# Mixture of experts in one fused block: the experts' leftover rows in units of 32 instead of 64

## The chip, the cores and the metric

The kernel runs on one core of a Trainium2 chip, as one program. Its time is device time in microseconds (us), the median of three runs; less is better. Times inside the kernel come from one profiled execution. PE is the matrix engine, DVE the vector engine, ACT the scalar engine, POOL the GpSimd engine, SP the queue that issues most transfers.

## The reference, cut to what matters

x is (32, 64, 256), which is 2048 tokens of 256 numbers. All arithmetic is float32.

```python
gate = xn @ wg_W + wg_b + (cond @ gg_W + gg_b)      # 8 experts
cw = top-2 of softmax(gate), as a weight per expert
h1 = relu(x @ W1[e] + b1[e])                        # 256 -> 512
h2 = relu(h1 @ W2[e] + b2[e])                       # 512 -> 512
out_e = h2 @ W3[e] + b3[e]                          # 512 -> 256
m = sum over e of cw[e] * out_e
x = x + attention_1(m)                              # 16 heads of 64, tanh, causal
x = x + ffn(attention_2(x))                         # second attention, then a quantized layer
```

Every token goes through two of eight experts, so there are 4096 (token, expert) rows to compute. How many each expert gets is known only at run time.

## The kernel before

**Stages.** After a short set-up (gate, ranks of the rows, a slot for each row) the expert stage runs over tiles of 128 slots; then the two attentions and the quantized layer run over 16 token tiles. The change lies in the expert stage and in the slot arithmetic ahead of it.

**Tiles.** The program's length is fixed, so there must be enough tiles for the worst split of the 4096 rows. There are `FULL` = 33 full tiles with one expert each and `MIXED` = 3 mixed tiles, each of `UNITS` = 2 units of `UNIT` = 64 rows, every unit with its own expert. `SLOT_TILES` = 36 tiles in all. They run in program order by position; `mixed(p)`, `nth(p)` and `slot_tile(p)` translate a position. The mixed tiles are at positions 13, 14 and 15.

**A full tile** keeps weights as the stationary operand and streams the 128 rows: layer 1 is 8 matrix products (L766), layer 2 is 16 (L796), layer 3 is 4 (L830, rows stationary, 256 columns streamed). A float32 product appears as two records in the trace. `turn_x` (L745) transposes the gathered rows.

**A mixed tile** has the rows of a unit as the stationary operand (64 columns of the array) and streams that unit's weights, 512 or 256 columns. The two units have their own column groups of the array (`tile_position=(0, g * UNIT)`), at L760, L790 and L816. Biases differ by row, so DVE adds gathered bias rows (L1934, L1942) and PE transposes the sum back (L775, L805).

**Order on PE.** A step j of `expert_step` is layer 1 of tile j+1, `turn_x` of tile j+2, layer 2 of tile j, layer 3 of tile j-1, with `turn_h2(j - 1)` and `turn_h1(j + 1)` where those tiles are mixed.

**Order on DVE.** In step j, DVE copies the expert's W1 for tile j+2 out of the arena (`take_w1`, L1910; L1906 when mixed), its W2 for tile j+1 (`take_w2`, L1926; L1921 when mixed), does the second activation (`relu2`, L1951) and adds b3 (L1970). A mixed tile needs the copies once per unit. ACT copies W3 for the units (`take_w3`).

**Transfers.** SP loads the attention weights (4 MB, L556) into the space that the mixed tiles' copies use, so it waits for the third layer of the last mixed tile: `sp.wait_ge(y_ps, LAST_MIXED + 1)`. PE waits for them (`w1_loaded`) after step `LAST - 2`. POOL gathers x rows (four buffers) and the mixed tiles' bias rows.

Of the kernel before, what the change touches and what calls it, by code (L numbers as in the profile page):

```python
# [35 lines left out]
UNIT = 64  # L36
UNITS = P // UNIT
FULL = 33
# [7 lines left out]
def units_left(small):  # L46

    blocks = (TOPK * TOK + (EXP - small) * (UNIT - 1) - small) // P
    return UNITS * max(blocks - FULL, 0) + max(small - max(FULL - blocks, 0), 0)  # L50

MIXED = -(-max(units_left(small) for small in range(EXP + 1)) // UNITS)
HOST = -(-(TOPK * TOK - EXP * UNIT) // P)
# [18 lines left out]
XG = 4  # L73
# [8 lines left out]
ROWS = dict(bo=HID, bout=HID, bffn=HID, bc2=H2, delta=1)  # L82
# [39 lines left out]
def mixed(p):  # L122

    return FIRST_MIXED <= p <= LAST_MIXED

def nth(p):

    return p - FIRST_MIXED if mixed(p) else p if p < FIRST_MIXED else p - MIXED

def slot_tile(p):

    if p < EXP:
        return p
    if p < FIRST_MIXED:
        return HOST + p - EXP
    return FULL + nth(p) if mixed(p) else nth(p) - (FULL - HOST)

# [25 lines left out]
def build(nc, t_in, out):  # L166
    ctx = ExitStack()
    with ctx:
# [19 lines left out]
        half_rows = sb("half_rows", [P, half_n])  # L188
# [24 lines left out]
        y = sb("y", [P, HID])  # L213
        root_table = sb("root_table", [P, 1])

        col = lambda name: cols[:, col_off[name][0]:col_off[name][1]]
        row = lambda name: rows[:, row_off[name][0]:row_off[name][1]]
        half_row = lambda name: half_rows[:, half_off[name][0]:half_off[name][1]]
# [41 lines left out]
        count_i, full_i, up_i = (r(EXP).bitcast(I32) for _ in range(3))  # L260
        past_first, past_full, to_first, to_full, to_rest, jump = (r(EXP) for _ in range(6))
        seg, room, behind = r(3 * EXP + 1), r(1), r(EXP)
        rank, over_first, over_full = (r(TT, EXP) for _ in range(3))
        picked = [over_first, over_full]
        slot_f = r(TOPK, TT)
# [12 lines left out]
        r = Region(l1_weights, 0, 4 * L1_SIZE)  # L278
# [11 lines left out]
        starts, row_slot, row_segment = r(3 * EXP + 1), r(MIXED), r(MIXED)  # L290
        starts_le, row_starts_le = r(FULL, 3 * EXP), r(MIXED, 3 * EXP)
# [7 lines left out]
        w1_b, w2_b = r(KH, MID), r(KM, MID)  # L299
        w3_now = [r(KM, HID) for _ in range(UNITS)]  # L300
        h1_rows, h2_rows = r(MID), r(MID)
        b1_rows, b2_rows = ([r(MID) for _ in range(BIAS_BUFS)] for _ in range(2))
        w1_of, w2_of = (w1_now, w1_b), (w2_now, w2_b)
# [20 lines left out]
        x_in = r(HID)  # L324
        wq2, wk2, wv2 = r(KH, HID), r(KH, HID), r(KH, HID)
# [179 lines left out]
        b1_gathered = [sem(f"b1_gathered{n}") for n in range(BIAS_BUFS)]  # L505
        b2_gathered = [sem(f"b2_gathered{n}") for n in range(BIAS_BUFS)]
# [12 lines left out]
        def _(sp):  # L519
# [29 lines left out]
            for half in range(2):  # L549
                sp.dma_start(half_rows[half * SEQ:(half + 1) * SEQ, :],  # L550
                             t_in["half_rows"][half:half + 1, :].to_broadcast([SEQ, half_n])).then_inc(half_loaded, 16)
# [7 lines left out]
            sp.wait_ge(w1_set, SLOT_TILES)  # L559
            for dst, name in ((wq2, "wq2"), (wk2, "wk2"), (wv2, "wv2"), (wc1, "wc1"), (wout2, "wout2")):  # L560
                sp.dma_start(dst, t_in[name].rearrange("(k p) n -> p k n", p=P)).then_inc(l2w_loaded, 16)
# [16 lines left out]
        def _(pool):  # L578
# [17 lines left out]
            for half in range(2):  # L596
                if half:
# [6 lines left out]
            pool.iota(row_slot, pattern=[[P, MIXED]], base=FULL * P, channel_multiplier=1,  # L604
                      allow_small_or_imprecise_dtypes=True).then_inc(row_slot_set, 1)
            pool.wait_ge(ids_set, 1)

            for j in range(SLOT_TILES):
# [5 lines left out]
                if mixed(j - 2):  # L615
                    n = nth(j - 2)
                    if n == 0:
                        pool.wait_ge(row_expert_set, 1)
                        pool.wait_ge(setup_done, 1)
                        pool.wait_ge(fa_stored, 16)  # L620
                    if n >= BIAS_BUFS:
                        pool.wait_ge(h1r_set, n - BIAS_BUFS + 1)
                    pool.indirect_dma_start(
                        out=b1_rows[n % BIAS_BUFS], out_offset=None, in_=t_in["b1"],
                        in_offset=bass.IndirectOffsetOnAxis(ap=row_expert[:, n:n + 1], axis=0)).then_inc(b1_gathered[n % BIAS_BUFS], 16)
                if mixed(j - 4):
                    n = nth(j - 4)
                    if n >= BIAS_BUFS:
                        pool.wait_ge(h2r_set, n - BIAS_BUFS + 1)
                    pool.indirect_dma_start(  # L630
                        out=b2_rows[n % BIAS_BUFS], out_offset=None, in_=t_in["b2"],
                        in_offset=bass.IndirectOffsetOnAxis(ap=row_expert[:, n:n + 1], axis=0)).then_inc(b2_gathered[n % BIAS_BUFS], 16)
# [3 lines left out]
            for t in range(TT):  # L636
# [7 lines left out]
                for c in range(TOPK):  # L644
                    pool.indirect_dma_start(  # L645
                        out=yg[:, c, :], out_offset=None, in_=expert_out if t else expert_out[0:(LAST_MIXED + 1) * P, :],
                        in_offset=bass.IndirectOffsetOnAxis(ap=slot_of[:, c, t:t + 1], axis=0)).then_inc(y_gathered, 16)
# [13 lines left out]
            for t in range(TT - 3, TT):  # L661
# [3 lines left out]
                pool.tensor_tensor(x1_bias[t % 2], x1, row("bffn"), ALU.add).then_inc(x1_bias_set, 1)  # L665
# [3 lines left out]
        def _(pe):  # L669
# [78 lines left out]
            def layer1(j):  # L748
# [21 lines left out]
            def turn_h1(j):  # L770
# [3 lines left out]
                for m in range(KM):  # L774
                    last = pe.transpose(ps[:, 1, m * P:(m + 1) * P], h1_rows[:, m * P:(m + 1) * P], ident[:, :])  # L775
                last.then_inc(h1r_turned, 1)

            def layer2(j):
# [7 lines left out]
                if mixed(j):  # L786
                    for k in range(KM):
                        for g in range(UNITS):
                            part_ = slice(g * UNIT, (g + 1) * UNIT)
                            last = mm(ps[part_, 2, :], h1_t[j % 2][:, k, part_], w2_of[g][:, k, :],  # L790
                                      start=k == 0, stop=k == KM - 1, tile_position=(0, g * UNIT))
# [8 lines left out]
            def turn_h2(j):  # L800
# [3 lines left out]
                for m in range(KM):  # L804
                    last = pe.transpose(ps[:, 3, m * P:(m + 1) * P], h2_rows[:, m * P:(m + 1) * P], ident[:, :])  # L805
                last.then_inc(h2r_turned, 1)

            def layer3(j):
                if mixed(j):
# [3 lines left out]
                    for k in range(KM):  # L813
                        for g in range(UNITS):
                            part_ = slice(g * UNIT, (g + 1) * UNIT)
                            last = mm(ps[part_, 4, 0:HID], h2_t[j % 2][:, k, part_], w3_now[g][:, k, :],  # L816
                                      start=k == 0, stop=k == KM - 1, tile_position=(0, g * UNIT))
# [3 lines left out]
                if j == EXP:  # L821
# [295 lines left out]
            def end_out1(t):  # L1117
# [4 lines left out]
                mm(dst, first_row, row("bo"), start=True, stop=False)  # L1122
# [91 lines left out]
            def end_out2(t):  # L1214
# [4 lines left out]
                mm(dst, first_row, row("bout"), start=True, stop=False)  # L1219
# [122 lines left out]
        def _(act):  # L1342
# [37 lines left out]
            def relu1(j):  # L1380
# [6 lines left out]
                if j == EXP:  # L1387
# [23 lines left out]
            def take_w3(j):  # L1411
# [4 lines left out]
                act.wait_ge(y_ps, j)  # L1416
                for g in range(UNITS):
                    e = act.value_load(row_expert[g * UNIT:g * UNIT + 1, nth(j):nth(j) + 1], min_val=0, max_val=EXP - 1)
                    at = act.snap(e * E_SIZE + W3_AT)
                    last = act.copy(w3_now[g].rearrange("p k n -> p (k n)"), arena[:, bass.ds(at, KM * HID)])  # L1420
                last.then_inc(w3_set, 1)

            def store_y(j):
                act.wait_ge(y_set, j + 1)
                act.dma_start(expert_out[j * P:(j + 1) * P, :], y[:, :]).then_inc(y_stored, 16)
# [296 lines left out]
        def _(dve):  # L1722
# [87 lines left out]
            first_row, seg_of = excl[:, :, 0], [seg[:, n * EXP + 1:(n + 1) * EXP + 1] for n in range(3)]  # L1810
            start_of, blocks_end = [starts[:, n * EXP:(n + 1) * EXP] for n in range(3)], starts[:, 2 * EXP:2 * EXP + 1]
# [3 lines left out]
            step(ts(count_i, up_i, -UNIT, None, ALU.bitwise_and))  # L1815
            step.go(ts(seg_of[0], full_i, float(P), None, ALU.min))
            step(tt(seg_of[2], count_i, full_i, ALU.subtract))
            step.go(tt(seg_of[1], full_i, seg_of[0], ALU.subtract))
            step(tt(rank, ps[:, 2, 0:TT * EXP].rearrange("p (i e) -> p i e", e=EXP), excl.rearrange("p e i -> p i e"), ALU.add))
            step.go(dve.tensor_tensor_scan(starts, seg, scan_zero.rearrange("p e i -> p (e i)")[:, 0:3 * EXP + 1], 0.0, ALU.add, ALU.add))  # L1820
            step.go(tt(past_full, full_i, first_row, ALU.add))
            step(ts(past_first, first_row, float(P), None, ALU.add))
            step.go(ts(room, blocks_end, -1.0 / UNITS, float(FULL * UNIT), ALU.mult, ALU.add))
            step.go(stt(to_full, start_of[1], -float(P), start_of[0], ALU.add, ALU.subtract))
            step.go(tt(to_first, start_of[0], first_row, ALU.subtract))
            step.go(tt(to_rest, full_i, start_of[0], ALU.add))
            step(tt(over_first, rank, per_e(past_first), ALU.is_ge))
            step.go(stt(behind, start_of[2], blocks_end, room.to_broadcast([P, EXP]), ALU.subtract, ALU.min))
            step.go(stt(jump, seg_of[0], 1.0 / P, to_full, ALU.mult, ALU.mult))
            step(tt(over_full, rank, per_e(past_full), ALU.is_ge))  # L1830
            step.go(stt(start_of[2], behind, 0.0, start_of[2], ALU.max, ALU.add))
            step.go(tt(to_rest, to_rest, jump, ALU.add))
# [615 lines left out]
```

## Time and profile before

| what | value |
|---|---|
| median of 3 runs | 742.73 us (741.77 to 743.66) |
| profiled execution, its own time | 744.68 us |
| span of its trace | 743.2 us |
| PE busy | 713.3 us (96%) |
| DVE, ACT, POOL busy | 65%, 39%, 12% |
| mean granted clock of PE | 0.986 of full speed |

The span runs from the first to the last instruction; the execution's own time holds what lies around it. A time by which a stage becomes shorter or longer can be taken from either.

### The profile page before, as it was taken

Reading aid. Unit: us, or ns where it says so; the run is one execution under the profiler, and the core shown is the slowest. Engines: PE = TensorE matmul, PEld = TensorE weight load, DVE = VectorE, ACT = ScalarE, POOL = GpSimd, SP = SyncE. Lnnn points to the kernel's source line nnn. Section 1 sums busy time; section 2 is a strip of 40 time slices with the busy share of each in tenths; the row PEclk is TensorE's granted clock in tenths of the full one; section 3 lists DMA queues with packets and bytes.
Section 4 is the critical chain, followed back from the end, with each engine's and each line's share of the span. In section 5 each row is a group of like instructions: output and inputs, shape, how many; then the busy total and the mean of one; then the engine's idle time right before and its main releaser. Section 6 shows DMA issues by size and latency. Waiting matters only on the chain.

```text
span 743.2 us, 20463 instructions
## 1 busy us (share of the span) xinstructions
PE 713.3 (96%) x8266; PEld 615.5 (83%) x8266; DVE 486.3 (65%) x1036; ACT 287.8 (39%) x839; POOL 90.9 (12%) x102
## 2 busy tenths in 40 slices
PE   6389999999999999999999999999999999999997
PEld 4279999559999999978778878978888897888785
DVE  4756565743545444334777787787778778777867
ACT  3032121142121221253465446445544654564552
POOL 2121112411111101031101101110110111000000
PEclk9599999999999999999999999999999999999999
DMA  7998111217111102310001000000110010000000
GB/s 262 336 353 322 37 37 56 81 43 257 50 37 37 37 30 69 118 50 23 16 9 30 30 7 25 30 23 10 30 31 9 23 30 24 8 16 16 9 9 23
DMA packets 21402, 49.13 MB, mean 66 GB/s; under 512 B 3323, under 2 KB 14971, under 8 KB 18749
## 3 DMA queue, kind: packets, MB, share of 16 engines
q1 hardware_dynamic: 12256, 32.47, 12.2%
q0 software_dynamic: 3744, 10.49, 4.7%
q10 hardware_dynamic: 5309, 4.87, 2.0%
q8 instruction: 66, 1.08, 0.6%
q14 instruction: 27, 0.22, 0.1%
HBM read 41.00 MB, written 6.82 MB: 64 GB/s over the span
## 4 chain that ended last, share of the span: by engine, by line
PE 94%; DVE 3%; ACT 1%; issue 1%; another core or an unknown queue 0%; DVEq 0%; POOL 0%; ACTq 0%; POOLq 0%
PE ps L897 16%; PE ps L796 15%; PE ps L766 8%; PE ps L923 8%; PE ps L830 7%; PE ps L982 7%; PE ps L948 4%; PE ps L998 3%; PE ps L941 2%; PE ps L973 2%; PE ps L1013 2%; PE ps L1075 2%; PE ps L1032 2%; PE ps L790 1%; PE ps L676 1%; PE ps L1045 1%
## 5 line engine op out<-in xcount | busy, mean ns | idle before, releaser
L897 PE MATMUL ps<-arena,l_weights 128*128 128x128 f32 x1024 | 125.9, 277 | 0.5 <-ACT arena L1470 0.5
L796 PE MATMUL ps<-h_t,w_now 128*128 128x128 f32 x1056 | 123.4, 275 | 1.2 <-DVE h_t L1951 1.2
L796 PEld LDWEIGHTS ps<-h_t,w_now 128*128 128x128 f32 x1056 | 120.5, 192 | 1.4 <-issue 1.4
L897 PEld LDWEIGHTS ps<-arena,l_weights 128*128 128x128 f32 x1024 | 119.3, 192 | 2.3 <-ACT arena L1470 1.0
L1395 ACT ACTIVATE h_t<-ps,cols 128x128 f32<-128x128 f32 x132 | 37.8, 367 | 163.9 <-PE ps L766 149.5
L1926 DVE COPY w_now<-arena 128x2048 f32 x33 | 40.5, 1227 | 83.2 <-PE ps L796 74.7
L1476 ACT ACTIVATE arena<-ps,cols 128x128 f32<-128x128 f32 x256 | 73.9, 387 | 48.0 <-PE ps L897 48.0
L645 POOL DMA_INDIRECT arena<-expert_out,slot_of x32 | 33.1, 1033 | 323.0 <-DVE arena L1979 272.8
L766 PEld LDWEIGHTS ps<-xg_t,w_now 128*128 128x128 f32 x528 | 63.4, 192 | 6.0 <-ACT xg_t L1378 3.5
L766 PE MATMUL ps<-xg_t,w_now 128*128 128x128 f32 x528 | 65.0, 276 | 3.0 <-ACT xg_t L1378 3.0
L612 POOL DMA_INDIRECT xg<-in_x,slot_tok x36 | 41.6, 1155 | 186.4 <-PE ps L745 157.4
L830 PE MATMUL ps<-arena,h_t 128*128 x264 | 62.5, 380 | 0.0
L923 PE MATMUL ps<-l_weights,arena 128*64 128x512 f32 x256 | 61.8, 605 | 0.0
L830 PEld LDWEIGHTS ps<-arena,h_t 128*128 128x128 f32 x264 | 47.7, 191 | 5.1
L982 PE MATMUL ps<-l_weights,arena 128*128 128x256 f32 x224 | 51.5, 383 | 0.0
L982 PEld LDWEIGHTS ps<-l_weights,arena 128*128 128x128 f32 x224 | 41.5, 190 | 5.2
L1910 DVE COPY w_now<-arena 128x1024 f32 x33 | 22.9, 694 | 29.3 <-PE ps L766 20.7
L1951 DVE TENSOR_SCALAR h_t<-ps,cols 128x128 f32<-128x128 f32 x128 | 35.8, 342 | 4.6 <-PE ps L796 4.5
L948 PE MATMUL ps<-ident,arena 128*128 128x128 f32 x256 | 38.3, 273 | 0.1
L2097 DVE TENSOR_TENSOR arena<-ps,half_rows 128x512 f32<-128x512 f32 x32 | 21.9, 686 | 22.7 <-PE ps L973 17.2
L923 PEld LDWEIGHTS ps<-l_weights,arena 128*64 128x64 f32 x256 | 15.6, 136 | 22.5 <-issue 21.4
L1559 ACT ACTIVATE arena<-arena 128x512 f32<-128x512 f32 x32 | 20.2, 631 | 31.6 <-DVE arena L2180 31.6
(366 smaller groups left out, 1097.1 us busy)
## 6 DMA issues: line engine op xcount, KB each, us to landing
arena<-in_experts SPq DMA_DIRECT2D x16, 1024.0 KB
expert_out<-y ACTq DMA_DIRECT2D x36, 128.0 KB
arena<-in_x_t SPq DMA_DIRECT2D x2, 1024.0 KB, 6.2
arena<-in_x SPq DMA_DIRECT2D x16, 128.0 KB
out<-arena SPq DMA_DIRECT2D x16, 128.0 KB, 1.7
b<-in_b SPq DMA_DIRECT2D x1, 1024.0 KB
l_weights<-in_wq SPq DMA_DIRECT2D x1, 1024.0 KB
l_weights<-in_wk SPq DMA_DIRECT2D x1, 1024.0 KB
```

What stands on the lines that cost most here:

```text
L612: pool.indirect_dma_start(out=xg[j % XG][:, :], out_offset=None, in_=t_in["x"], in_offset=bass.IndirectOffsetOnAxis(ap=slot_tok[:, slot_ti ...
L766: last = mm(ps[:, 0, m * P:(m + 1) * P], w1_now[:, k, m * P:(m + 1) * P], xg_t[:, k, :], start=k == 0, stop=k == KH - 1)
L796: last = mm(ps[:, 2, m * P:(m + 1) * P], w2_now[:, k, m * P:(m + 1) * P], h1_t[j % 2][:, k, :], start=k == 0, stop=k == KM - 1)
L830: last = mm(bank(4, HID), h2_t[j % 2][:, k, :], flat[:, bass.ds(at + k * HID, HID)], start=k == 0, stop=k == KM - 1)
L897: last = mm(ps[:, b, c * P:(c + 1) * P], wt[:, k, f:f + P], m_t[:, k, :], start=k == 0, stop=k == KH - 1)
L923: last = mm(ps[r * SEQ:(r + 1) * SEQ, value_bank(t, s), :], m_t[:, k, s * SEQ:(s + 1) * SEQ], wv[:, k, r * 512:(r + 1) * 512], start=k == ...
L948: last = pe.transpose(bank_[:, m * P:(m + 1) * P], p[:, h:h + 2, :], ident[:, :])
L982: last = mm(bank(1, HID), ctx_t[:, c, :], wo[:, c, :], start=c == 0, stop=c == C1 - 1)
L1395: last = f(h1_t[j % 2][:, k, :], ps[:, 0, k * P:(k + 1) * P], ACT.Relu, bias=cols[:, bass.ds(e * KM + at + k, 1)])
L1476: last = f(dst[:, cc, :], ps[:, project_bank(t, n), c * P:(c + 1) * P], ACT.Tanh, bias=col(bias)[:, cc:cc + 1])
L1926: dve.tensor_copy(w2_now[:, :, :].rearrange("p k n -> p (k n)"), arena[:, bass.ds(at, KM * MID)]).then_inc(w2_set, 1)
L1951: last = ts(h2_t[j % 2][:, k, :], ps[:, 2, k * P:(k + 1) * P], cols[:, bass.ds(e * KM + at + k, 1)], 0.0, ALU.add, ALU.max)
```

## The change

The leftover rows are handled in units of 32. There are 28 full tiles and 6 mixed ones, 34 in all. A mixed tile has three units, `UNIT_ROWS`: rows 0 to 63 (a couple, one expert), rows 64 to 95 and rows 96 to 127 (singles, each with an expert). Mixed tiles stand at positions 13, 16, 19, 22, 25 and 28. The couple's weights are copied where a tile's weights were before; the singles' weights are copied earlier, at the end of three steps (`spare_w1`, `spare_w2` twice). The slot arithmetic handles four segments rather than three. The bias rows have one buffer rather than two each, x rows three rather than four, and two small tables of rows (`half_rows`, `token_rows`) are loaded after the expert stage's last W1 copy.

```diff
-UNIT = 64
-UNITS = P // UNIT
-FULL = 33
+UNIT, COUPLE = 32, 64
+UNIT_ROWS = [slice(0, COUPLE), slice(COUPLE, COUPLE + UNIT), slice(COUPLE + UNIT, P)]
+FULL = 28
...
-FIRST_MIXED = EXP + FULL - HOST
-LAST_MIXED = FIRST_MIXED + MIXED - 1
-BIAS_BUFS = 2
+FIRST_MIXED = 13
+MIXED_POSITIONS = [FIRST_MIXED + 3 * n for n in range(MIXED)]
+LAST_MIXED = MIXED_POSITIONS[-1]
...
-XG = 4
+XG = 3
...
             def layer1(j):
...
                 if mixed(j):
+                    pe.wait_ge(spare_set, 3 * nth(j) + 1)
                     for k in range(KH):
-                        for g in range(UNITS):
-                            part_ = slice(g * UNIT, (g + 1) * UNIT)
+                        for g, part_ in enumerate(UNIT_ROWS):
                             last = mm(ps[part_, 0, :], xg_t[:, k, part_], w1_of[g][:, k, :],
-                                      start=k == 0, stop=k == KH - 1, tile_position=(0, g * UNIT))
+                                      start=k == 0, stop=k == KH - 1, tile_position=(0, part_.start))
...
             def expert_step(j):
...
                 if exists(j - 1, SLOT_TILES):
                     add_b3(j - 1)
+                spare_w1(j + 3)
+                spare_w2(j + 2, 1)
+                spare_w2(j + 1, 2)
...
+            def spare_w1(j):
+                if not mixed(j):
+                    return
...
+                experts_of[j] = [unit_expert(j, g) for g in range(len(UNIT_ROWS))]
+                for g in (1, 2):
+                    at = dve.snap(experts_of[j][g] * E_SIZE + W1_AT)
+                    last = dve.tensor_copy(w1_of[g].rearrange("p k n -> p (k n)"), arena[:, bass.ds(at, KH * MID)])
+                last.then_inc(spare_set, 1)
+
+            def spare_w2(j, g):
...
+                at = dve.snap(experts_of[j][g] * E_SIZE + W2_AT)
+                dve.tensor_copy(w2_of[g].rearrange("p k n -> p (k n)"), arena[:, bass.ds(at, KM * MID)]).then_inc(spare_set, 1)
...
-            step(dve.tensor_copy(slot_of[:, :, :], slot_f))
+            step(ts(past_split, slot_f, -float(SPLIT_AT), 0.0, ALU.add, ALU.max))
+            step.go(ts(shift_back, past_split, float(SPLIT * COUPLE), float(COUPLE - 2 * SPLIT * COUPLE), ALU.is_ge, ALU.mult))
+            step(ts(chunk_at, past_split, -COUPLE, None, ALU.bitwise_and))
+            step(tt(slot_f, slot_f, shift_back, ALU.add))
+            step(tt(slot_of[:, :, :], slot_f, chunk_at, ALU.add))
```

On PE, the second mixed tile of before (position 14, step 14) read as follows: its transposes, then layer 2 with `w_now` for one unit and `l_weights` for the other, both with 64 output rows.

```order
L745 MATMUL ps<-ident,xg 128x128 x2
L805 MATMUL ps<-ident,l_weights 128x128 x4
L790 MATMUL ps<-w_now,h_t 64x512
L790 MATMUL ps<-l_weights,h_t 64x512
L790 MATMUL ps<-w_now,h_t 64x512
L790 MATMUL ps<-l_weights,h_t 64x512
L790 MATMUL ps<-w_now,h_t 64x512
L790 MATMUL ps<-l_weights,h_t 64x512
L790 MATMUL ps<-w_now,h_t 64x512
L790 MATMUL ps<-l_weights,h_t 64x512
L775 MATMUL ps<-ident,l_weights 128x128 x4
```

The changed kernel has this at the first mixed tile (position 13, step 13):

```order
L774 MATMUL ps<-xg_t,w_now 128x128 x8
L753 MATMUL ps<-ident,xg 128x128 x2
L798 MATMUL ps<-w_now,h_t 64x512
L798 MATMUL ps<-l_weights,h_t 32x512 x2
L798 MATMUL ps<-w_now,h_t 64x512
L798 MATMUL ps<-l_weights,h_t 32x512 x2
L798 MATMUL ps<-w_now,h_t 64x512
L798 MATMUL ps<-l_weights,h_t 32x512 x2
L798 MATMUL ps<-w_now,h_t 64x512
L798 MATMUL ps<-l_weights,h_t 32x512 x2
```

Where products of one width followed each other, a product 64 wide and two 32 wide now alternate.

On DVE, the end of step 14 and the start of step 15 in the changed kernel hold the three-part b3 addition of tile 13 (L1999), a spare W2 copy for tile 16 (L1966), that tile's b1 addition (L1974) and the next copies (`w_now` is the tile's own weights, `l_weights` a spare):

```order
L1999 ISA
L1999 TENSOR_TENSOR y<-ps,b 32x256
L1966 ISA
L1966 COPY l_weights<-arena 128x2048
L1974 TENSOR_TENSOR mixed_rows<-ps,bias_rows 128x512
L1905 TENSOR_LOAD tile_expert
L1905 ISA x2
L1925 ISA
L1926 ISA
L1926 COPY w_now<-arena 128x1024
L1936 ISA
L1936 COPY w_now<-arena 128x2048
```

Before, the same kind of place (around the first mixed tile's b1 addition, L1934) had both units' copies one behind the other:

```order
L1934 TENSOR_TENSOR l_weights<-ps,l_weights 128x512
L1887 TENSOR_LOAD row_expert
L1887 ISA x2
L1887 TENSOR_LOAD row_expert
L1887 ISA x2
L1906 ISA
L1906 COPY w_now<-arena 128x1024
L1906 ISA
L1906 COPY l_weights<-arena 128x1024
L1921 ISA
L1921 COPY w_now<-arena 128x2048
L1921 ISA
```

A spare's copy moved from between the step's own work to the step's end.

## Rows read from the trace of the kernel before

**Rows 1.** The page, part 1: busy time of each engine

```profile
PE 713.3 (96%) x8266; PEld 615.5 (83%) x8266; DVE 486.3 (65%) x1036; ACT 287.8 (39%) x839; POOL 90.9 (12%) x102
```

**Rows 2.** Waits of PE, whole span: total, times, longest

```profile
PE ps L725 <- DVE arena L1860: 10.9, 2, 10.4
...
PE ps L766 <- ACT xg_t L1378: 3.0, 2, 1.7
...
PE ps L796 <- DVE h_t L1951: 1.2, 1, 1.2
```

**Rows 3.** Timeline, one step of full tiles: start, duration, engine, line

```profile
260.22 1.95 PE L766 MATMUL ps<-xg_t,w_now 128*128 128x128 f32 x16
...
262.23 3.74 PE L796 MATMUL ps<-h_t,w_now 128*128 128x128 f32 x32
...
265.80 1.89 PE L830 MATMUL ps<-arena,h_t 128*128 x8
266.30 1.23 DVE L1926 COPY w_now<-arena 128x2048 f32 x1 [3.19 <-PE ps L796]
...
267.53 1.95 PE L766 MATMUL ps<-xg_t,w_now 128*128 128x128 f32 x16
268.48 0.41 DVE L1970 TENSOR_TENSOR y<-ps,b 128x256 f32<-128x256 f32 x1
```

**Rows 4.** Windows: the five steps 12 to 16, with three mixed tiles

```profile
130.13:172.46 42.33, 41.10 (x268) 25.19 (x267) 24.10 (x38) 13.10 (x25) 11.93 (x9) 1.00 0.19 61
```

**Rows 5.** Timeline of PE and its weight loads, mixed tile at position 14

```profile
150.37 0.65 PE L790 MATMUL ps<-w_now,h_t 128*64 128x512 f32 x1
...
150.38 0.64 PE L790 MATMUL ps<-l_weights,h_t 128*64 128x512 f32 x1
...
153.00 0.59 PE L790 MATMUL ps<-w_now,h_t 128*64 128x512 f32 x1
...
153.43 0.59 PE L790 MATMUL ps<-w_now,h_t 128*64 128x512 f32 x1
...
153.96 0.42 PEld L775 LDWEIGHTS ps<-ident,l_weights 128*128 128x128 f32 x4 [0.81 <-issue]
...
154.55 1.95 PE L816 MATMUL ps<-l_weights,h_t 128*64 128x256 f32 x16
156.42 2.05 PE L766 MATMUL ps<-xg_t,w_now 128*128 128x128 f32 x16
```

**Rows 6.** Timeline: a change from 64-wide products to 64 by 64 tiles

```profile
407.74 1.03 PE L923 MATMUL ps<-l_weights,arena 128*64 128x512 f32 x4
408.70 0.32 PEld L973 LDWEIGHTS ps<-arena 64*64 64x64 f32 x16 [0.81 <-issue]
```

**Rows 7.** 32-wide products in four column groups: timeline; group over the span

```profile
7.38 1.07 PE L687 MATMUL ps<-arena 128*32 128x512 f32 x8
...
L1066 PE MATMUL ps<-arena 128*32 128x64 f32 x416 | 8.5, 222 | 0.0
```

**Rows 8.** Timeline of DVE in the slot arithmetic, where PE waits

```profile
22.67 0.16 DVE L1825 TENSOR_TENSOR arena<-l_weights,arena 128x8 f32<-128x8 f32 x1
22.75 0.16 DVE L1826 TENSOR_TENSOR arena<-arena,l_weights 128x8 f32<-128x8 int32 x1
...
24.25 0.28 DVE L1835 TENSOR_TENSOR arena<-arena 128x128 f32<-128x128 f32 x1
24.57 0.29 DVE L1836 TENSOR_TENSOR arena<-arena 128x128 f32<-128x128 f32 x1
...
26.47 0.18 DVE L1845 CAST slot_of<-arena 128x32 int32<-128x32 f32 x1
26.68 0.18 DVE L1850 TENSOR_SCALAR arena<-slot_of 128x32 int32<-128x32 int32 x1
```

**Rows 9.** SP's first issue of attention weights; transfer rates from 184 us, slices of 0.2 us

```profile
172.63 0.39 SPq L556 DMA_DIRECT2D l_weights<-in_wq  x1
...
GB/s 369 348 353 415 333 328 348 338 359 389 451 241 41 41 26 61 26 26 20 0 0 0 0 0 0 0 0 0 169 364 123 0 0 0 0 0 0 82 246 225
```

More of the change, by code:

```diff
@@ L122, in mixed, with out_block @@
 def mixed(p):
-    return FIRST_MIXED <= p <= LAST_MIXED
+    return p in MIXED_POSITIONS
 def nth(p):
-    return p - FIRST_MIXED if mixed(p) else p if p < FIRST_MIXED else p - MIXED
+    before = sum(at < p for at in MIXED_POSITIONS)
+    return before if mixed(p) else p - before
 def slot_tile(p):
[L135 to L139, printed above, removed]
+    return FULL + nth(p) if mixed(p) else nth(p)
+def out_block(p):
+    return p if p < EXP else EXP + nth(p) if mixed(p) else MIXED + nth(p)
 def later(t):
@@ L298, in build @@
         r = Region(l1_weights, 0, 4 * L1_SIZE)
[L299 to L303, printed above, removed]
+        w2_b, w2_c = r(KM, MID), r(KM, MID)
+        w3_of = [r(KM, HID), r(KM, HID), w3_c]
+        w1_b, w1_c = r(KH, MID), r(KH, MID)
+        w1_of, w2_of = (w1_now, w1_b, w1_c), (w2_now, w2_b, w2_c)
         class Blocks:
@@ L324, in build @@
         x_in = r(HID)
+        token_rows, half_rows = r(token_n), r(half_n)
         wq2, wk2, wv2 = r(KH, HID), r(KH, HID), r(KH, HID)
@@ L504, in build @@
         row_expert_set = sem("row_expert_set")
-        b1_gathered = [sem(f"b1_gathered{n}") for n in range(BIAS_BUFS)]
-        b2_gathered = [sem(f"b2_gathered{n}") for n in range(BIAS_BUFS)]
+        b1_gathered = sem("b1_gathered")
+        b2_gathered = sem("b2_gathered")
+        spare_set = sem("spare_set")
         w3_set = sem("w3_set")
@@ L559, in _ @@
             sp.wait_ge(w1_set, SLOT_TILES)
+            for half in range(2):
+                sp.dma_start(half_rows[half * SEQ:(half + 1) * SEQ, :],
+                             t_in["half_rows"][half:half + 1, :].to_broadcast([SEQ, half_n])).then_inc(half_loaded, 16)
+            sp.dma_start(token_rows, t_in["token_rows"].to_broadcast([P, token_n])).then_inc(half_loaded, 16)
             for dst, name in ((wq2, "wq2"), (wk2, "wk2"), (wv2, "wv2"), (wc1, "wc1"), (wout2, "wout2")):
@@ L664, in _ @@
                 pool.wait_ge(x1_bias_set, t)
-                pool.tensor_tensor(x1_bias[t % 2], x1, row("bffn"), ALU.add).then_inc(x1_bias_set, 1)
+                pool.tensor_tensor(x1_bias[t % 2], x1, token_row("bffn"), ALU.add).then_inc(x1_bias_set, 1)
         @block.tensor
@@ L813, in layer3 @@
                     for k in range(KM):
[L814 to L817, printed above, removed]
+                        for g, part_ in enumerate(UNIT_ROWS):
+                            last = mm(ps[part_, 4, 0:HID], h2_t[j % 2][:, k, part_], w3_of[g][:, k, :],
+                                      start=k == 0, stop=k == KM - 1, tile_position=(0, part_.start))
                     last.then_inc(y_ps, 1)
@@ L1121, in end_out1 @@
                 dst = bank(O_END[t], HID)
-                mm(dst, first_row, row("bo"), start=True, stop=False)
+                mm(dst, first_row, token_row("bo"), start=True, stop=False)
                 for c in range(C1):
@@ L1218, in end_out2 @@
                 dst = bank(OUT2_END[t], HID)
-                mm(dst, first_row, row("bout"), start=True, stop=False)
+                mm(dst, first_row, token_row("bout"), start=True, stop=False)
                 for c in range(C2):
@@ L1415, in take_w3 @@
                     act.wait_ge(moe_loaded[1], 16 * EXP)
-                act.wait_ge(y_ps, j)
-                for g in range(UNITS):
-                    e = act.value_load(row_expert[g * UNIT:g * UNIT + 1, nth(j):nth(j) + 1], min_val=0, max_val=EXP - 1)
+                if nth(j):
+                    act.wait_ge(y_ps, MIXED_POSITIONS[nth(j) - 1] + 1)
+                for g, part_ in enumerate(UNIT_ROWS):
+                    row_ = part_.start
+                    e = act.value_load(row_expert[row_:row_ + 1, nth(j):nth(j) + 1], min_val=0, max_val=EXP - 1)
                     at = act.snap(e * E_SIZE + W3_AT)
-                    last = act.copy(w3_now[g].rearrange("p k n -> p (k n)"), arena[:, bass.ds(at, KM * HID)])
+                    last = act.copy(w3_of[g].rearrange("p k n -> p (k n)"), arena[:, bass.ds(at, KM * HID)])
                 last.then_inc(w3_set, 1)
@@ L1886, in unit_expert @@
             def unit_expert(j, g):
-                return dve.value_load(row_expert[g * UNIT:g * UNIT + 1, nth(j):nth(j) + 1], min_val=0, max_val=EXP - 1)
+                row_ = UNIT_ROWS[g].start
+                return dve.value_load(row_expert[row_:row_ + 1, nth(j):nth(j) + 1], min_val=0, max_val=EXP - 1)
             def take_w1(j):
-                if j == EXP:
+                if nth(j) == EXP and not mixed(j):
                     dve.wait_ge(experts_set, 2)
@@ L1918, in take_w2 @@
                 if mixed(j):
-                    for g in range(UNITS):
-                        at = dve.snap(experts_of[j][g] * E_SIZE + W2_AT)
-                        last = dve.tensor_copy(w2_of[g][:, :, :].rearrange("p k n -> p (k n)"), arena[:, bass.ds(at, KM * MID)])
-                    last.then_inc(w2_set, 1)
+                    at = dve.snap(experts_of[j][0] * E_SIZE + W2_AT)
+                    dve.tensor_copy(w2_now[:, :, :].rearrange("p k n -> p (k n)"), arena[:, bass.ds(at, KM * MID)]).then_inc(w2_set, 1)
                     return
@@ L1926, in take_w2 @@
                 dve.tensor_copy(w2_now[:, :, :].rearrange("p k n -> p (k n)"), arena[:, bass.ds(at, KM * MID)]).then_inc(w2_set, 1)
+            def spare_w1(j):
+                if not mixed(j):
+                    return
+                if nth(j) == 0:
+                    dve.wait_ge(row_expert_set, 1)
+                    for n in range(2):
+                        dve.wait_ge(moe_loaded[n], 16 * EXP)
+                else:
+                    dve.wait_ge(l1_ps, MIXED_POSITIONS[nth(j) - 1] + 1)
+                experts_of[j] = [unit_expert(j, g) for g in range(len(UNIT_ROWS))]
[4 more added lines that the diff above has]
+            def spare_w2(j, g):
+                if not mixed(j):
+                    return
+                if nth(j) == 0:
+                    dve.wait_ge(setup_done, 1)
+                    dve.wait_ge(fa_stored, 16)
+                else:
+                    dve.wait_ge(l2_ps, MIXED_POSITIONS[nth(j) - 1] + 1)
+                at = dve.snap(experts_of[j][g] * E_SIZE + W2_AT)
+                dve.tensor_copy(w2_of[g].rearrange("p k n -> p (k n)"), arena[:, bass.ds(at, KM * MID)]).then_inc(spare_set, 1)
             def add_b1(j):
@@ L2128, in l1_bias_o @@
                 dve.wait_ge(o_ps, t + 1)
-                tt(o_rows, bank(1, HID), row("bo"), ALU.add).then_inc(ob_set, 1)
+                tt(o_rows, bank(1, HID), token_row("bo"), ALU.add).then_inc(ob_set, 1)
             def l1_residual(t):
@@ L2145, in l2_x1_bias @@
                     dve.wait_ge(fin_set, t - 1)
-                tt(x1_bias[t % 2], x1, row("bffn"), ALU.add).then_inc(x1_bias_set, 1)
+                tt(x1_bias[t % 2], x1, token_row("bffn"), ALU.add).then_inc(x1_bias_set, 1)
             def l2_z(t):
@@ L2218, in l2_bias_a @@
                 dve.wait_ge(a_ps, t + 1)
-                tt(a_rows, bank(6, HID), row("bout"), ALU.add).then_inc(a_set, 1)
+                tt(a_rows, bank(6, HID), token_row("bout"), ALU.add).then_inc(a_set, 1)
             def l2_scales(t):
@@ L2416 @@
         parity=np.stack([(np.arange(P) // D2 % 2 == odd).astype(np.float32) for odd in range(2)], axis=1))
-    rows = dict(bo=a(L0_attn_bo), bout=a(L0_cond2_bout),
-                bffn=a(L0_ffn_bias), bc2=a(L0_cond2_bc2)[order], delta=a(L0_ffn_delta_act))
+    token_rows = dict(bo=a(L0_attn_bo), bout=a(L0_cond2_bout), bffn=a(L0_ffn_bias))
+    rows = dict(bc2=a(L0_cond2_bc2)[order], delta=a(L0_ffn_delta_act))
     half_rows = dict(bv=a(L0_attn_bv).reshape(2, -1), bv2=bqkv[2].reshape(HALF, 2, D2).transpose(1, 0, 2).reshape(2, -1))
@@ L2432 @@
         "cols": join(cols, COLS, 1), "aug": join(aug, AUG, 1),
-        "rows": join(rows, ROWS, 0)[None], "half_rows": join(half_rows, HALF_ROWS, 1), "setup_rows": join(setup_rows, SETUP_ROWS, 0)[None],
+        "rows": join(rows, ROWS, 0)[None], "token_rows": join(token_rows, TOKEN_ROWS, 0)[None],
+        "half_rows": join(half_rows, HALF_ROWS, 1), "setup_rows": join(setup_rows, SETUP_ROWS, 0)[None],
         "we2_t": c(a(L0_cond2_We2).T), "ffn_w": c(a(L0_ffn_weight)), "ffn_dw": c(a(L0_ffn_delta_w).reshape(HID, NBLK)),
```

164 lines of the change are left out of this document (84 added, 80 removed).

## The prediction

> **What bounds the kernel now.** I read the busy shares first: PE is busy for 713.3 of 743.2 us [rows 1]. Then its waits: after the set-up almost nothing holds it. The one long wait, 10.4 us, is for DVE's slot arithmetic before any tile can start; two waits for the first gathered rows follow, and a single one of 1.2 us for DVE's activation in the expert stage [rows 2]. So two things count: how many PE microseconds the expert stage takes, and how long the slot arithmetic is. All other engines matter only where they come late for PE.
>
> The timeline of a step of full tiles shows what one costs: layer 1 starts at 260.22 and the next step's at 267.53, so 7.31 us a tile, with no gap on PE [rows 3]. The stretch with the mixed tiles took 42.33 us for five steps [rows 4]. Five full steps would be 36.55, so three mixed tiles cost 5.78 us more. PE's 1.23 us of idle time (42.33 minus 41.10 busy) is the wait of rows 2; the other 4.55 us are work, 1.52 us a mixed tile, mostly the transposes. The matrix products themselves are no dearer than a full tile's, because both units stream at once: the two records of L790 start at 150.37 and 150.38, and the next ones come 0.43 us apart (153.00, 153.43), which is a 512-column record [rows 5].
>
> **Fewer tiles.** 36 become 34: 2 x 7.31 = 14.6 us less [rows 3]. Three more tiles are mixed, 3 x 1.52 = 4.55 us more [rows 4]. The 1.2 us wait came from both units' copies standing ahead of a full tile's activation; that order is gone, so 1.2 us less, between 0 and that. Together -11.3 us if three units stream abreast as two do.
>
> **The slot arithmetic** lies on PE's long wait, so every operation added counts in full. Added are about five operations of 8 columns at 0.08 us (L1825 to L1826), three of 128 columns at up to 0.32 (L1835 to L1836), and four of 32 columns, three of them chained at 0.21 (L1845 to L1850) [rows 8]: 0.4 + 0.8 + 0.7 = 1.9 us. The bounds are 1.2 (all overlapped by half more) and 2.5.
>
> **Spare copies on DVE.** In a full step W2's copy starts 6.08 us after the step, lasts 1.23, then the activation and b3 follow until 8.7 (268.48 + 0.41 against 260.22) [rows 3]. A spare W2 copy behind that ends near 9.9 to 10.2. The tile ahead of a mixed one has its step lengthened to about 8.0 by `turn_h1`, and PE wants the spare 2.0 us (262.23 - 260.22) into the next one, at 10.0. So each of six mixed tiles may wait 0 to 0.3 us: 1.0 us in all. If that cover were gone the whole copy would show, 6 x 1.23 = 7.4 us, the upper bound; the lower is 0. Behind a spare W1 pair or the longer b3 of a mixed tile stands only the next W1 copy, which has over 2 us to spare. ACT's W3 copies for three units now wait for the mixed tile before, far back, rather than for the tile just ended, and cost nothing.
>
> **Transfers.** The 4 MB of attention weights used to start at 172.63 and were needed 120 us later. The rates fall to 41 GB/s 2.4 us into the window from 184, at 186.4, so the load takes 13.8 us [rows 9]. It now starts after layer 3 of position 28, in step 29, and PE waits for it after step 31: 2 x 7.31 = 14.6 us of cover. Slack is 0.8 us. Two row gathers ran beside it before, none does now, but two gathers for the first attention tile fall into its end. I take 0.2 us, with 0 and 3 (a fifth slower) as bounds. `half_rows` and `token_rows`, 0.7 MB, are about 2 us at these rates and have the last two expert steps as cover: nothing, or 2 us without it. On POOL the b2 gather waits for the b1 addition, with x gathers queued behind it; those are issued three steps (22 us) before their use, so nothing.
>
> **The width of the products.** Before, neighbours inside a mixed layer were all 64 wide. Now the order is 64, 32, 32 for each k. No row shows widths in alternation, so I bound it. From below: four 32-wide groups stream abreast (8 records in 1.07 us, two rounds of 0.43 plus the end), and weight loads with their products go by in 0.02 us each (8.5 us for 416) [rows 7]. By these rows three units cost what two do: +0.
>
> From above, changes of shape elsewhere. The last 64-wide records start at 153.43, and nothing of L775 (128 wide) starts until 153.96, its weight load included, though inside L790 loads run ahead of their turn. That is 0.43 of streaming and then 0.10. From 64-wide products to 64 by 64 tiles the same: four records from 407.74 are two rounds, the last at 408.17, and the next weight load comes at 408.70 after 0.81 us without one [rows 5, 6]. So in both rows PE let the products in flight run out before it began another shape. If 64 beside 32 is such a change, the couple streams alone, then the singles:
>
> - a k of layers 1 and 2 (512 columns, two records): 2 x (0.86 + 0.10) = 1.92 us instead of 0.86, six times a tile: 6.4 us
> - a k of layer 3 (L816: 1.87 us for four, 0.47 each [rows 5]): 2 x (0.47 + 0.10) = 1.14 instead of 0.47, four times: 2.7 us
>
> 9.1 us a tile, 54 us for six. The records of two units start in turns there, not by k [rows 5]; if the shape changes with every record, it is 12 x (0.43 + 0.20) + 8 x (0.23 + 0.20) = 11.0 us a tile, 66 us. I take the middle, 60 us. Between the ends, 0 and 66, this is the value of the nearest rows: every change of shape I looked at empties the array, and the zero rests on rows of one width only.
>
 The trace agrees for other pairs of shapes (0.10 us beyond the streaming time) and shows nothing on this pair. By that rule the widths' share of the sum would be +60; by the abreast rows +0.
>
> **Sum.** -14.6 + 4.55 - 1.2 + 1.9 + 0.2 + 60 = +50.8 us (the spare copies then have longer steps to hide in). Against the profiled execution's own 744.68 that is 795.5; the median of runs is 1.95 lower: **793.5 us**, 742.73 + 50.8.
>
> **The rivals.**
>
> *Three units abreast* (chance 0.35). For it: two 64-wide and four 32-wide groups stream together, at disjoint columns, and a couple and singles are at disjoint columns too. Against it: rows 5 and 6. Time: -14.6 + 4.55 - 1.2 + 1.9 + 1.0 + 0.2 = -8.2, so **734.5 us**, range 732 to 739 by the bounds above. This is the case on the other side. It decides at 1.4 us a mixed tile (8.2 / 6), 0.07 us for each of 20 rounds of records.
>
> *Gaps without serial streaming* (0.12). The loads lose their lead at each change of width, 0.10 us, but the products in flight overlap. By k that is 20 gaps a tile, by record 40: 120 or 240 gaps, 12 or 24 us on top of 734.5: 746 to 758.
>
> *The copies are late as well*: DVE's spare copies exposed in full add 6.4 us to the abreast case, the late weights up to 3 us: 744 at worst. I count it inside the abreast case's upper tail.
>
> **How the numbers follow.** Array emptied at each change of width: 0.53, own range 779 to 805. Abreast 0.35, gaps only 0.12. A measurement of this kernel can tell about 0.3%, 2.2 us, from no change: below 740.5 is faster, above 745.0 slower. Faster: 0.33 of the abreast case. Same: 0.03 (abreast with late copies, or gaps smaller than thought). Slower: 0.64. The two main cases lie on either side, so the range must reach from the one to the other: 733 to 805 leaves out some 0.1 at the low end and under 0.1 above.
>
> **What would show it.** In the profile of the changed kernel, L798's 64-wide and 32-wide records starting at the same time with 0.43 us to the next would refute the forecast and give 734 or so. Records of one width starting only when the other's are through, mixed tiles of some 17 to 19 us of PE time and a span near 790, would confirm it. PE's waits for the slot arithmetic should grow from 10.4 to about 12.3, and no wait of PE for L1966 should exceed 0.3 us. PE waiting for the weights' load after step 31 by more than 1 us would show that term wrong. The prediction fails most simply if widths at disjoint columns do not count as a change of shape.

## The result, and the profile after

The changed kernel takes **791.05 us** (median of 4 runs, 790.85 to 791.36) beside 743.19 us for the kernel before (median of 4, 741.77 to 745.83). The ratio is 1.0646, with an interval of 1.0632 to 1.0661: 6.5% slower, 47.9 us. The forecast was 793.5 us. Beside experiments 1 to 4 the kernel before ran thirteen times: twelve runs have a median of 742.52 us (741.63 to 743.75), and the thirteenth, 829.41 us at a granted clock of 0.843, is in the chip's slow state and is left out of every comparison. Beside experiments 5 and 6 its median is 742.83 us (seven runs).

The busy times on the page of the changed kernel:

```profile
span 789.6 us, 20385 instructions
PE 758.6 (96%) x8246; PEld 596.4 (76%) x8246; DVE 503.2 (64%) x1055; ACT 297.3 (38%) x835; POOL 90.9 (12%) x108
```

PE has 20 records fewer than in [rows 1] and is busy 45.3 us longer, while the span grows by 46.4. So the time is not a new wait: PE's own work became longer. The waits of PE (us in total, times, longest) say the same:

```profile
PE ps L733 <- DVE arena L1883: 12.6, 2, 12.1
...
PE ps L774 <- DMA l_weights<-in_wo: 1.2, 1, 1.2
```

The first answers to the wait for the slot arithmetic in [rows 2], 1.7 us longer. The last is new. No wait for a spare copy (L1966) or for an activation in the expert stage is in the list.

The timeline of PE without its weight loads, in layer 2 of the first mixed tile, where `w_now` is the couple's weights and `l_weights` the singles':

```profile
143.98 1.04 PE L798 MATMUL ps<-w_now,h_t 128*64 128x512 f32 x2
144.95 1.05 PE L798 MATMUL ps<-l_weights,h_t 128*32 128x512 f32 x4
145.93 1.07 PE L798 MATMUL ps<-w_now,h_t 128*64 128x512 f32 x2
146.94 1.05 PE L798 MATMUL ps<-l_weights,h_t 128*32 128x512 f32 x4
147.92 1.07 PE L798 MATMUL ps<-w_now,h_t 128*64 128x512 f32 x2
```

This is the place to read. A k is one of the 128-deep slices that a layer sums over, with one product of each unit. A round is the 0.43 us in which one 512-column record streams. In [rows 5] the two 64-wide products start 0.01 us apart, and each next pair comes 0.43 us later. Here the two singles start together (four records in 1.05 us), but only 0.97 us after the couple's start, and the next couple 0.98 us after theirs. Each width takes two rounds of 0.43 plus 0.11 to 0.15 us, by itself. A k of 512 columns is 1.95 to 1.99 us instead of 0.86. In layer 3, with 256 columns, one k is 1.13 to 1.14 us instead of 0.47 (starts of two neighbouring k's; `x3` are the couple's two 64-wide records, printed together with the first 32-wide one of a single):

```profile
159.82 0.98 PE L823 MATMUL ps<-l_weights,h_t 128*64 128x256 f32 x3
...
160.96 0.98 PE L823 MATMUL ps<-l_weights,h_t 128*64 128x256 f32 x3
```

The weight loads tell how the turn is taken. Each row is the load that goes with the products starting at the same time:

```profile
144.95 0.14 PEld L798 LDWEIGHTS ps<-l_weights,h_t 128*32 128x32 f32 x4 [0.81 <-issue]
145.93 0.19 PEld L798 LDWEIGHTS ps<-w_now,h_t 128*64 128x64 f32 x2 [0.84 <-issue]
```

Before each change of width the loader stands idle for 0.81 to 0.84 us, about as long as the products in flight stream, as it did ahead of L775 in [rows 5]. It does not load the other width while products of the first are in flight, although the two have column groups of their own.

A window over the three steps with the first mixed tile (stretch, length, then busy time of PE, PEld, DVE, ACT and POOL with counts, granted clock, DMA share, GB/s):

```profile
131.71:164.35 32.64, 32.52 (x187) 18.69 (x186) 14.77 (x27) 7.32 (x16) 5.26 (x5) 1.00 0.15 41
```

Three full steps are 3 x 7.31 = 21.93 us, so the mixed tile costs 10.7 us more than a full one. Before it was 1.52. The clock is the full one in this stretch as it was in [rows 4], so it has no part in this.

### The profile page after: what moved, and what is told of

Read it like the earlier page. It is cut to its first block, busy times and chain, and to the rows that moved or that the text cites. A ratio compares the mean times of both kernels' runs of the same rounds, so it can differ in the third digit from the quotient of the medians.

```text
span 789.6 us, 20385 instructions
## 1 busy us (share of the span) xinstructions
PE 758.6 (96%) x8246; PEld 596.4 (76%) x8246; DVE 503.2 (64%) x1055; ACT 297.3 (38%) x835; POOL 90.9 (12%) x108
## 4 chain that ended last, share of the span: by engine, by line
PE 92%; DVE 3%; DMA 3%; ACT 1%; issue 0%; SPq 0%; ACTq 0%
PE ps L904 15%; PE ps L804 12%; PE ps L930 8%; PE ps L989 6%; PE ps L798 6%; PE ps L774 6%; PE ps L837 6%; PE ps L823 3%; PE ps L955 3%; PE ps L1005 3%; PE ps L768 3%; PE ps L948 2%; PE ps L980 2%; DMA l_weights<-in_wo 2%; PE ps L1020 2%; PE ps L1082 2%
## 5 line engine op out<-in xcount | busy, mean ns | idle before, releaser
L804 PE MATMUL ps<-h_t,w_now 128*128 128x128 f32 x896 | 104.6, 275 | 0.0
L804 PEld LDWEIGHTS ps<-h_t,w_now 128*128 128x128 f32 x896 | 102.3, 192 | 0.0
L1402 ACT ACTIVATE h_t<-ps,cols 128x128 f32<-128x128 f32 x112 | 32.0, 367 | 100.3 <-PE ps L774 89.3
L1940 DVE COPY w_now<-arena 128x2048 f32 x28 | 34.4, 1227 | 44.2 <-PE ps L804 36.3
L1385 ACT COPY xg_t<-ps 128x256 f32<-128x256 f32 x34 | 12.9, 381 | 123.3 <-PE ps L753 123.3
L774 PE MATMUL ps<-xg_t,w_now 128*128 128x128 f32 x448 | 55.2, 276 | 3.2 <-ACT xg_t L1385 1.9
L774 PEld LDWEIGHTS ps<-xg_t,w_now 128*128 128x128 f32 x448 | 53.8, 192 | 5.6 <-ACT xg_t L1385 2.4
L837 PE MATMUL ps<-arena,h_t 128*128 x224 | 53.6, 382 | 0.0
L837 PEld LDWEIGHTS ps<-arena,h_t 128*128 128x128 f32 x224 | 40.4, 190 | 9.4 <-issue 5.0
L2137 DVE TENSOR_TENSOR arena<-ps,arena 128x512 f32<-128x512 f32 x32 | 22.0, 686 | 22.7 <-PE ps L980 17.2
```

The lines of the kernel that those rows point to most:

```text
L774: last = mm(ps[:, 0, m * P:(m + 1) * P], w1_now[:, k, m * P:(m + 1) * P], xg_t[:, k, :], start=k == 0, stop=k == KH - 1)
L804: last = mm(ps[:, 2, m * P:(m + 1) * P], w2_now[:, k, m * P:(m + 1) * P], h1_t[j % 2][:, k, :], start=k == 0, stop=k == KM - 1)
L837: last = mm(bank(4, HID), h2_t[j % 2][:, k, :], flat[:, bass.ds(at + k * HID, HID)], start=k == 0, stop=k == KM - 1)
L1940: dve.tensor_copy(w2_now[:, :, :].rearrange("p k n -> p (k n)"), arena[:, bass.ds(at, KM * MID)]).then_inc(w2_set, 1)
```

## The experiments

The theory: products 64 and 32 wide never stream together, and every change of width lets the array run empty, so a mixed tile has its streaming twice and a small gap besides. Rivals: it is the three experts or the 32-wide products themselves that are dear; or the change itself costs a fixed time, and the streams would overlap.

**1. The kernel before with one alternation put in.** Tiles, order, copies and transfers stay. The second unit's product is issued as two 32-wide ones, the first unit's stays 64 wide. The same edit was made in all three layers.

```diff
+MM_ROWS = [(0, slice(0, 64)), (1, slice(64, 96)), (1, slice(96, P))]
...
-                        for g in range(UNITS):
-                            part_ = slice(g * UNIT, (g + 1) * UNIT)
+                        for g, part_ in MM_ROWS:
                             last = mm(ps[part_, 2, :], h1_t[j % 2][:, k, part_], w2_of[g][:, k, :],
-                                      start=k == 0, stop=k == KM - 1, tile_position=(0, g * UNIT))
+                                      start=k == 0, stop=k == KM - 1, tile_position=(0, part_.start))
```

> The kernel before, with one edit: in its three mixed tiles the second unit's product of 64 rows is issued as two of 32 rows with the same weights, so that widths alternate 64, 32, 32 as in the change. Nothing else moves. Theory (a change of width empties the array, so the 64-wide and the 32-wide products stream one after the other): each mixed tile costs 9.4 us more of PE, as in the changed kernel's trace, 28 us in all, 771 us. Rival (only a gap of 0.1 us at each of 20 changes a tile, products overlap): 6 us more, 749. Rival (widths are harmless, the change's cost is its copies and slots): 743, within 1 us.

Measured: 770.77 us, ratio 1.0381 (1.0364 to 1.0399) to a before of 742.52. That is 28.2 us for three mixed tiles, 9.4 each. In its timeline the alternation reads just as in the changed kernel:

```profile
144.38 1.07 PE L789 MATMUL ps<-w_now,h_t 128*64 128x512 f32 x2
145.38 1.05 PE L789 MATMUL ps<-l_weights,h_t 128*32 128x512 f32 x4
146.36 1.07 PE L789 MATMUL ps<-w_now,h_t 128*64 128x512 f32 x2
```

Two experts, no spare copies, the old positions, and still the whole cost. The alternation alone is enough.

**2. The kernel before, 32-wide throughout.** The same edit with four 32-wide products in place of two 64-wide; the cut below is against experiment 1.

```diff
-MM_ROWS = [(0, slice(0, 64)), (1, slice(64, 96)), (1, slice(96, P))]
+MM_ROWS = [(0, slice(0, 32)), (0, slice(32, 64)), (1, slice(64, 96)), (1, slice(96, P))]
```

> The kernel before, with both units' products of 64 rows issued as two of 32 rows each: one width, 32, in the whole mixed layer, and twice the instructions. Theory: four column groups stream abreast, no change inside a layer, 743 us within 1 us. Rival (32-wide products are dear in themselves, by their number or their weight loads): as slow as the alternating one or between, 749 to 771.

Measured: 743.22 us (ten runs, 741.56 to 747.97), ratio 1.0011 (0.9993 to 1.0030), no difference. Twice as many products and weight loads in the mixed layers cost nothing that these runs can tell, so it is not the 32-wide product that is dear.

**3. The changed kernel, 32-wide throughout.** The couple is issued as two 32-wide products with the same weights.

```diff
+MM_ROWS = [(0, slice(0, 32)), (0, slice(32, 64)), (1, slice(64, 96)), (2, slice(96, P))]
...
-                        for g, part_ in enumerate(UNIT_ROWS):
+                        for g, part_ in MM_ROWS:
```

> The changed kernel with the couple's product of 64 rows issued as two of 32 rows with the same weights, so that all products of a mixed layer are 32 wide. Copies, slots, biases and order stay. Theory: the 1.98 us of a k at 512 columns goes back to 0.86 and the 1.13 us at 256 columns to 0.47, 9.4 us a tile, 56 us for six: 791 - 56 = 735, and the late spare copies may show 1 us: 734 to 737. Rival (the array is not the cause, the copies of three units or the late loads are): above 780. Rival (three streams of different weights cannot all be fed at once): between 745 and 780.

Measured: 735.20 us, ratio 0.9899 (0.9881 to 0.9917). One edit turns 6.5% slower into 1.0% faster. All four column groups start within 0.01 us, with three experts' weights, and the next round follows 0.42 us later:

```profile
141.68 0.62 PE L799 MATMUL ps<-w_now,h_t 128*32 128x512 f32 x2
141.69 0.62 PE L799 MATMUL ps<-l_weights,h_t 128*32 128x512 f32 x2
142.11 0.62 PE L799 MATMUL ps<-w_now,h_t 128*32 128x512 f32 x2
```

The window over the same three steps is 9.23 us shorter than the changed kernel's, with 20 more PE records:

```profile
131.53:154.94 23.41, 23.29 (x207) 17.96 (x210) 13.78 (x24) 7.33 (x16) 5.49 (x5) 1.00 0.22 58
```

A mixed tile with three experts is thus 23.41 - 21.93 = 1.48 us dearer than a full one, as before with two ([rows 4]: 1.52). The rival of three dear experts is out.

**4. The changed kernel with its products grouped by width.** In each mixed layer the couple's products for all k come first, then the singles'. Inside a layer the width then changes once, where with alternation over n slices (2, 4 and 4 in the three layers) it changes 2n - 1 times: 3 such changes a tile and not 3 + 7 + 7 = 17. All products stay as they were.

```diff
+WIDTHS = [[(0, UNIT_ROWS[0])], [(1, UNIT_ROWS[1]), (2, UNIT_ROWS[2])]]
...
-                    for k in range(KM):
-                        for g, part_ in enumerate(UNIT_ROWS):
+                    for width in WIDTHS:
+                      for k in range(KM):
+                        for g, part_ in width:
```

> The changed kernel with each mixed layer ordered by width: the couple's products for all k first (64 wide), then both singles' for all k (32 wide). Changes of width fall from two a k to two a layer, 20 to 6 a tile; how much is streamed at each width is the same. Theory (serial streaming is the cost, the gap a small part): 14 changes of 0.1 us fewer a tile, 8 us in all, 783 us. Rival (the change of width itself is the cost): 14 of 20 parts of 48 us come back, 757 us or less.

Measured: 779.94 us, ratio 1.0503 (1.0486 to 1.0521), 3 us below the 783 expected, most of it because a change costs more than the 0.1 us assumed. Its timeline shows both widths streaming at full rate, one behind the other:

```profile
142.82 3.62 PE L801 MATMUL ps<-w_now,h_t 128*64 128x512 f32 x8
146.37 3.63 PE L801 MATMUL ps<-l_weights,h_t 128*32 128x512 f32 x16
149.92 1.99 PE L841 MATMUL ps<-arena,h_t 128*128 x8
```

3.55 us for eight rounds is 0.44 a round. This divides the cost in two. Fourteen changes fewer in each of six tiles gave 791.05 - 779.94 = 11.1 us, 0.13 us a change on average. The rest, 779.94 - 735.20 = 44.7 us, is the second stream, 6 x 0.86 + 4 x 0.47 = 7.04 us a tile, 42.2 for six, and besides it the three changes a tile that are left, 18 x 0.13 = 2.3. Fixed gaps without serial streaming would have ended near that rival's 757 or below; it is out.

**5. The alternation in layer 3 alone.** The kernel of experiment 3, with the couple 64 wide only in layer 3.

```diff
-                        for g, part_ in MM_ROWS:
+                        for g, part_ in enumerate(UNIT_ROWS):
                             last = mm(ps[part_, 4, 0:HID], h2_t[j % 2][:, k, part_], w3_of[g][:, k, :],
```

> The changed kernel with 32-wide products in layers 1 and 2 and the couple's 64-wide product beside two of 32 in layer 3 alone. Theory: only layer 3 pays, 4 x (1.13 - 0.47) = 2.65 us a tile, 16 us in all: 751 us. Rival (the cost is per change of width and equal for long and short streams): 8 of 20 changes a tile, 40% of 56 us = 22 us, 757 us.

Measured: 750.57 us (749.34 to 751.19), ratio 1.0102, against 735.20: 15.4 us, 2.56 a tile, 0.64 for each of 24 k's. At 256 columns a k costs 1.13 - 0.47 = 0.66 by the timeline; at 512 it costs 1.10. The cost goes down with the length of the stream, as it does if the streams are serial, and does not stay equal per change. The profile of experiment 3 holds a wait of 1.2 us for `in_wo` that this one does not, so the times show slightly too little; PE's busy time, which holds no waits, grew from 703.0 to 718.7 us, 15.7 us or 0.65 a k.

**6. A later wait for the attention weights.** The kernel of experiment 3, with PE's wait for the four transfers moved from after step 31 to just before the first attention product that uses them.

```diff
-            pe.wait_ge(w1_loaded, 16 * 4)
...
             layer3(LAST - 2)
+            pe.wait_ge(w1_loaded, 16 * 4)
             l1_q(0, 0)
```

> The changed kernel with 32-wide products throughout (735.2 us), and PE's wait for the attention weights moved from behind step 31 to just ahead of the first projection, past one layer 1, one layer 2, a transposition and one layer 3 (7.3 us of work). Theory (the 1.2 us wait on the load of the output weights is a plain lateness of the load): it goes, 734.0 us. Rival (the load's landing sets something else that is late as well, or the wait only moves to the first gathered rows): 735 us, no change.

Measured: 734.15 us (734.03 to 734.43), ratio 0.9884 (0.9868 to 0.9901), 1.05 below experiment 3, though the intervals of the two ratios overlap. The wait for `in_wo` is gone from PE's list. That the later place did it is not shown. The last transfer's time from issue to landing was 14.5 us in the changed kernel, 14.4 in experiment 3 and 14.6 in experiment 4, but less in the profiles of experiments 5 (first row) and 6:

```profile
l_weights<-in_wo SPq DMA_DIRECT2D x1, 1024.0 KB, 12.9
l_weights<-in_wo SPq DMA_DIRECT2D x1, 1024.0 KB, 12.1
```

In experiment 6 it was issued at 272.41, so it landed at 284.5, and PE came to the old place of the wait only at 285.49: it would not have waited there either. In experiment 5 the wait stood at its old place, and PE's list has no wait for `in_wo`.

This is the best of the kernels here: 8.7 us below the one before, 56.9 below the changed one.

## Why the prediction was right, point by point

The forecast was right in its main step: that a 64-wide product beside 32-wide ones is a change of shape that empties the array. That step was a choice between rows that spoke for either side, taken at 0.53 against 0.35, and the range of 733 to 805 us held the rival's 734.5 as well. That the measured time lies in the range says little; that it lies 2.5 us from the forecast is in part luck, because misses of both signs offset each other (below).

**The widths: 60 us taken, 56 measured.** Right in mechanism; the size was 4 us too high. The difference between the changed kernel and experiment 3 is 55.9 us, and the windows give 9.23 us a tile, 55.4 for six. Of the prediction's two ends it is the lower one, changes by k, that holds: a k at 512 columns 1.97 us where 1.92 was predicted, one at 256 columns 1.13 where 1.14 was. I had taken the middle to the reading by record, because in [rows 5] the two units start in turns. That turned out wrong: the two records of one product go in neighbouring rounds, and the width changes twice a k. The gap at a change is 0.13 us (experiment 4) where [rows 5] let me take 0.10.

What tipped the choice beforehand was to look at what the weight loader does at other changes of shape. The rows with four groups abreast [rows 7] were true as well (experiment 3 runs so) but were of one width.

**Fewer tiles, three more of them mixed, slot arithmetic: -14.6, +4.55, +1.9.** Experiment 3 is free of the widths and tests their sum. The slot arithmetic grew PE's wait by 1.7 us, a mixed tile cost 1.48 more, and the load 1.25: -14.6 + 4.5 + 1.7 + 1.25 = -7.2 us. Measured: 735.20 - 742.52 = -7.3 us.

**The 1.2 us wait: predicted gone, but not a property of the order.** It is absent after, but it is also absent from the profiles of experiments 1 and 2, whose DVE order is that of before. So nothing ties it to that order; it most likely belonged to the one profiled execution, which took 1.95 us more than the median. The same goes for 1.1 us of the wait for `xg_t`, 3.0 us in [rows 2] and 1.9 in every later profile. Counting it as a gain made the sum 1.2 us too low against the median. A short wait seen once in one profile should have had zero as its likelier value.

**Spare copies: 0 to 0.3 each, measured some 0.1, once.** The list of waits has no row for L1966 in the changed kernel, and none for the same copy in experiment 3, where the steps are short. In both kernels PE is idle for 0.12 us in the window of the first mixed tile, and its second layer starts 0.14 us after the spare copy ends (141.54 and 141.68 in experiment 3); in the later tiles it follows the transposes 0.16 us sooner. The cover that I worked out (copy done near 9.9 to 10.2, wanted at 10.0) was enough.

**The attention weights: 0.2 us taken, 1.25 measured, within the bounds of 0 to 3.** The load starts at 326.94 and PE waits until 342.90, 16.0 us where the 13.8 of [rows 9] were expected. Part of this is my reading of [rows 9]: 13.8 us is when the rate fell, not when the load ended. From 164 to 204 us in that trace the SP queue moved nothing but this load (1856 packets, 4.19 MB); 14 of the packets came after 186.4, the last near 187.3, 14.7 us after the start. Against 14.6 us of cover the slack was nothing, not 0.8. SP and POOL issues beside its end:

```profile
326.94 0.38 SPq L558 DMA_DIRECT2D l_weights<-in_wq  x1
...
337.09 1.16 SPq L563 DMA_DIRECT2D arena<-in_half_rows  x2
337.34 0.94 POOL L653 DMA_INDIRECT arena<-expert_out,slot_of  x1 [29.36 <-DVE w_now L1926]
...
342.90 0.82 PE L774 MATMUL ps<-xg_t,w_now 128*128 128x128 f32 x5 [1.25 <-DMA l_weights<-in_wo]
```

I had called `half_rows` covered by looking only at who reads it, and had taken the gathers as light. Both run beside the last third of the load. They do not account for the wait by themselves. From its first issue to its last landing the load took 15.9 us in the changed kernel and in experiment 3 and 16.1 in experiment 4, but 14.4 in experiment 5 and 13.5 in experiment 6, and in all five `half_rows` is issued 10.1 to 10.2 us after the load's start and the first gather 0.2 us later. What makes the difference stays open; the last two ran in a session of their own, each was profiled once, and no run took the neighbours away.

**The sum.** With the measured terms: -14.6 + 4.5 + 1.7 + 1.25 + 56 = +48.9 us; the medians differ by 47.9, so 1 us is left over. Against the profiled execution, which held the waits of 1.2 and 1.1 us of its own, it is 46.6, and the span grew by 46.4. The prediction's +50.8 had the widths 4 us too high, the load 1 us and the passing wait 1.2 us too low; the offsetting of these is the luck in its last figure.

**The pair of widths, which no row of before could show.** The loader idles 0.81 to 0.84 us at each change between 64-wide and 32-wide products, although their column groups are disjoint, and the two stream one after the other. The Trainium skill, page "TensorEngine Tiling (Array Packing)", section "Tiling Modes", says that a change of tiling mode drains TensorE, and lists 128x64 and 128x32 apart. The trace agrees. Experiments 2 and 3 are the other half of it: changing only the tile, within one mode, costs nothing here (743.22 beside 742.52 us in experiment 2).

## What to carry to other kernels

Give work that is packed side by side on the array one column width throughout: where a 64-wide and 32-wide products meet, issue the 64-wide one as two of 32 with the same weights, which cost nothing here. Before trusting "disjoint, so parallel", look at how far the weight loads run ahead at some other change of shape in the trace: a loader idle for as long as the products in flight stream was the sign, here, that the array is being emptied. And a large transfer that is moved towards its reader should be costed to its last packet, not to the fall of its rate, and with more slack than one profile seems to need: the same load took 13.5 to 16.1 us in five profiles.

## What was not expected of the hardware

- About three quarters of the price of mixing widths is serial streaming (42.2 of 55.9 us), and the rest is the 102 changes of width at 0.13 us each. Grouping by width therefore recovers only 11.1 us, equal widths 55.9.
- Four 32-wide column groups with three different experts' weights keep up a round of 0.43 us at 512 columns, and doubling the count of products and loads (experiment 2, 120 records more) changed the time by 0.1%, within its interval.
